# A graph layer's two projections regrouped: neighbour half alone first, self half beside each tile's aggregation

## The reference

```python
Wi, Wj = (W[:, :Din], W[:, Din:])
mi = jnp.einsum('bkd,od->bko', x, Wi)
mj = jnp.einsum('bkd,od->bko', x, Wj)
a = adj.astype(x.dtype)
deg = a.sum(axis=1)
out = deg[None, :, None] * (mi + b) + jnp.einsum('ij,bjo->bio', a, mj)
...
x = _layernorm(x + _L0_gnn_ref(x, adj, L0_gnn_W, L0_gnn_b), axis=-1)
```

## Time and profile before

| | |
|---|---|
| median of 3 runs | 1643.62 us (1643.59 to 1643.74) |
| the profiled execution, own time | 1643.72 us |
| its span in the profile | 1641.9 us |
| TensorE busy | 1634.2 us |
| VectorE, ScalarE, GpSimd busy | 844.8, 661.7, 498.4 us |
| moved by DMA | 187.27 MB |

### The profile page before, as it was taken

The page is one execution under the profiler, slowest core; times in us unless marked ns, Lnnn a source line. Parts: engine busy times, 40 slices in busy tenths (PEclk is TensorE's granted clock), DMA queues, the critical chain, the costliest instruction groups (busy, mean ns, idle before and its releaser), DMA issues.

```text
span 1641.9 us, 24654 instructions
## 1 busy us (share of the span) xinstructions
PE 1634.2 (100%) x7196; PEld 1346.8 (82%) x7196; DVE 844.8 (51%) x1879; ACT 661.7 (40%) x964; POOL 498.4 (30%) x386
## 2 busy tenths in 40 slices
PE   9999999999999999999999999999999999999998
PEld 6888888888888888888888888888888888888886
DVE  8787644554444544444544544444544454544544
ACT  5765445332453324532245332452325522255221
POOL 3532134311343114431144211442114421144210
PEclk9999999999999999999999999999999999999999
DMA  6676422332234323243223332233323333233332
GB/s 205 193 226 223 141 84 94 131 108 96 83 102 133 100 93 96 89 134 109 84 95 101 123 115 83 95 114 117 102 83 102 124 106 106 74 101 115 96 115 70
DMA packets 102843, 187.27 MB, mean 114 GB/s; under 512 B 11424, under 2 KB 11680, under 8 KB 102816
## 3 DMA queue, kind: packets, MB, share of 16 engines
q1 hardware_dynamic: 84672, 154.05, 29.1%
q10 hardware_dynamic: 18144, 32.91, 6.3%
HBM read 119.80 MB, written 67.11 MB: 114 GB/s over the span
## 4 chain that ended last, share of the span: by engine, by line
PE 98%; DVE 1%; DMA 0%; issue 0%; POOL 0%; ACT 0%; DVEq 0%
PE agg_ps L375 57%; PE cross_ps L343 14%; PE main_ps L351 14%; PE main_ps L353 14%; DVE W_lo L558 0%; DVE W_df L561 0%; DMA mi_in<-in_wt 0%; DVE adjT L555 0%; DVE x_raw L579 0%; DVE mj_lo L568 0%; PE deg_ps L360 0%; POOL x_df L281 0%; DVE x_top L576 0%; DVE stats L630 0%; DVE r L628 0%
## 5 line engine op out<-in xcount | busy, mean ns | idle before, releaser
L375 PE MATMUL agg_ps<-mj_hi,adjT 128*128 128x512 f32 x2048 | 797.0, 389 | 0.0
L375 PE MATMUL agg_ps<-mj_lo,adjT 128*128 128x512 f32 x2048 | 796.7, 389 | 0.0
L470 ACT ACTIVATE adjT<-adjT 128x2048 fp32r (+1 forms) x128 | 245.4, 1917 | 562.8 <-PE agg_ps L375 562.8
L375 PEld LDWEIGHTS agg_ps<-mj_hi,adjT 128*128 128x128 f32 x2048 | 384.5, 188 | 79.9
L375 PEld LDWEIGHTS agg_ps<-mj_lo,adjT 128*128 128x128 f32 x2048 | 384.3, 188 | 79.7
L351 PE MATMUL main_ps<-W_hi,x_hi 128*128 128x512 f32 x1008 | 392.3, 389 | 0.0
L353 PE MATMUL main_ps<-W_lo,x_lo 128*128 128x512 f32 x1008 | 392.1, 389 | 0.0
L292 POOL TENSOR_TENSOR mi_in<-mi_in,bias 128x512 f32<-128x512 f32 x128 | 166.9, 1307 | 649.9 <-DMA mi_in<-mi_dram 649.9
L628 DVE TENSOR_TENSOR r<-agg_ps,r 128x512 f32<-128x512 f32 x128 | 88.6, 692 | 355.0 <-PE agg_ps L375 354.9
L343 PE MATMUL cross_ps<-W_df,x_df 128*128 128x512 f32 x1008 | 270.2, 390 | 0.6 <-DVE W_df L561 0.5
L286 POOL TENSOR_TENSOR mj_lo<-mj,mj_hi 128x512 f32 (+1 forms) x126 | 166.7, 1323 | 323.4 <-ACT mj_hi L458 323.4
(11 more groups left out here) (59 smaller groups left out, 592.1 us busy)
## 6 DMA issues: line engine op xcount, KB each, us to landing
mi_dram<-mi SPq DMA_DIRECT2D x128, 256.0 KB, 2.1
mi_in<-mi_dram SPq DMA_DIRECT2D x128, 256.0 KB, 2.7
r<-in_x SPq DMA_DIRECT2D x128, 256.0 KB, 2.6
out<-r SPq DMA_DIRECT2D x127, 256.0 KB, 2.1
x_raw<-in_xt ACTq DMA_DIRECT2D x124, 256.0 KB, 2.7
adj_in<-in_adjt SPq DMA_DIRECT2D x64, 256.0 KB, 3.9
r<-in_wt SPq DMA_DIRECT2D x4, 256.0 KB, 5.2
adj_in<-in_xt SPq DMA_DIRECT2D x2, 256.0 KB, 4.0
```

The source lines that it names most:

```text
L375: last = nc.tensor.matmul(agg_ps[s][:, :], adjT[s][:, j, :], part[:, j, :], start=(j == 0 and part is mj_hi), stop=(j == NT - 1 and part i ...
L470: nc.scalar.activation(adjT[s][:, :, :], adjT8[:, :, bass.ds(i * P, P)], ACT.Copy).then_inc(adjT_ready, 1)
```

## The change

A batch becomes 32 steps (STEPS). Steps 0 to 15 project the neighbour half of tiles 0 to 15. Step 16 + i projects the self half of tile i, and the aggregation of tile i follows on TensorE at once. mi stays in SBUF, in two buffers; x is loaded and split once for each step, so twice a tile. x_hi is now ScalarE's rounding of x itself; VectorE makes the rest and x_df (two instructions with two SBUF operands), ScalarE x_lo; GpSimd keeps mj_lo and the bias. x_raw has four buffers, mj and cross two. Only the neighbour halves of tiles 0 and 1 are projected in plain fp32. W is rounded by ScalarE first; VectorE splits the self half of W at tiles 3, 5, 7 and 9 of batch 0. The adjacency comes by row tile, four chunks a tile, widened straight into adjT and kept as int8 afterwards (`keep`); one reduce and one fp32 matmul a tile give deg. The body of a batch, looped over batches 1 to 6, is written out without inner loops.

```diff
-            def store_mi(n):
-                sp.wait_ge(mi_ready, n + 1)
...
+                    sp.wait_ge(x_lo_ready, q)
+                    sp.wait_ge(x_df_ready, q)
+                    sp.dma_start(x_raw[(t + 5) % 4][:, :], xt[base + (t + 5) % NT]).then_inc(x_loaded[(t + 5) % 4], 16)
...
-            def difference(n, s):
-                pool.wait_ge(x_parts_ready, 2 * (n - NATIVE) + 2)
-                pool.tensor_tensor(x_df[s][:, :], x_top[:, :], x_lo[s][:, :].bitcast(fp32),
-                                   ALU.subtract).then_inc(x_df_ready, 1)
...
+            def add_bias(q, i):
+                pool.wait_ge(comb_ready, q + 1)
+                pool.tensor_tensor(mi[i % 2][:, :], mi[i % 2][:, :], bias[:, :], ALU.add).then_inc(mib_ready, 1)
...
+            def project(q, st, zero):
+                s = st % 2
+                half = 1 if st < NT else 0
...
+                pe.wait_ge(x_df_ready, q - NATIVE + 1)
+                if not (zero and st < 2 * NATIVE):
+                    pe.wait_ge(cross_ready, q - 2 * NATIVE + 1)
...
+            def degree(i):
+                pe.wait_ge(deg_part_ready, i + 1)
+                if i:
+                    pe.wait_ge(deg_ready, i)
+                nc.tensor.matmul(deg_ps[:, 0:2], deg_part[i % 2][:, :], ones[:, :],
+                                 start=True, stop=True).then_inc(deg_in_psum, 1)
...
+                        project(STEPS * bt + t, t, zero)
+                for i in range(NT):
+                    if zero:
+                        degree(i)
+                    project(STEPS * bt + NT + i, NT + i, zero)
+                    aggregate(bt, i, zero)
...
-            for h in range(2):
-                for n in range(NATIVE):
-                    project_native(n, h)
+            for n in range(NATIVE):
+                project_native(n)
...
+            def round_x(q, st, turn):
+                act.wait_ge(x_loaded[st % 4], turn)
+                act.wait_ge(main_done, q - 1)
+                nc.scalar.activation(x_hi[st % 2][:, :], x_raw[st % 4][:, :], ACT.Copy).then_inc(x_hi_ready, 1)
...
+            def scale_x(q, st):
+                act.wait_ge(x_rest_ready, q - NATIVE + 1)
+                nc.scalar.activation(x_lo[st % 2][:, :], x_raw[st % 4][:, :], ACT.Copy, scale=S).then_inc(x_lo_ready, 1)
...
+            def widen_chunk(c):
+                i, k = c // 4, c % 4
+                act.wait_ge(adj_loaded[c % AB], 16 * (c // AB + 1))
...
+                nc.scalar.activation(adjT[i % 2][:, 4 * k:4 * k + 4, :],
+                                            adj_in[c % AB][:, :].rearrange("p (a d) -> p a d", a=4),
+                                     ACT.Copy).then_inc(adj_wide, 1)
+
+            def keep(i):
+                act.wait_ge(adj_wide, 4 * i + 4)
+                nc.scalar.activation(adjT8[:, :, i * P:(i + 1) * P], adjT[i % 2][:, :, :].bitcast(fp32),
+                                     ACT.Copy).then_inc(adj_kept, 1)
...
-            copy_w_hi(0, DK)
+            round_x(2, 2, 16)
+            round_w(0)
+            scale_x(2, 2)
             native_mj_hi(1)
...
+            round_x(3, 3, 16)
+            for c in range(1, DK):
+                round_w(c)
+            act.wait_ge(w_ready, DK)
+            load_x(4, 4)
+            load_x(5, 5)
+            scale_x(3, 3)
...
+                def step(st, middle):
+                    q = first_step + st
+                    take_cross(q, st)
...
+                        round_x(q + 2, st + 2, x_turn(bt, st + 2))
+                    if middle:
+                        top_of_mj(q, st)
+                    if ahead:
+                        scale_x(q + 2, st + 2)
+                    if not middle and not (final and st + 5 >= STEPS):
+                        act.wait_ge(x_df_ready, q)
+                        load_x(base + (st + 5) % STEPS % NT + (NT if st + 5 >= STEPS else 0), st + 5)
...
+                    if zero:
+                        keep(i)
+                    if not (final and i >= NT - 2):
+                        act.wait_ge(agg_done, m + 1)
+                        if zero and i + 2 < NT:
+                            for k in range(3):
+                                widen_chunk(4 * (i + 2) + k)
                             root(m)
...
+                            widen_chunk(4 * (i + 2) + 3)
...
+            def split_x(q, st):
+                dve.wait_ge(x_hi_ready, q - NATIVE + 1)
+                nc.vector.tensor_tensor(x_raw[st % 4][:, :], x_raw[st % 4][:, :], x_hi[st % 2][:, :].bitcast(fp32),
                                         ALU.subtract).then_inc(x_rest_ready, 1)
...
+                dve.wait_ge(x_rest_ready, q - NATIVE + 1)
+                nc.vector.scalar_tensor_tensor(x_df[st % 2][:, :], x_raw[st % 4][:, :], -S,
+                                               x_hi[st % 2][:, :].bitcast(fp32),
+                                               ALU.mult, ALU.add).then_inc(x_df_ready, 1)
...
+            def combine(q, st, into):
+                dve.wait_ge(main_done, q + 1)
+                dve.wait_ge(cross_ready, q - NATIVE + 1)
...
+            def count(i):
+                dve.wait_ge(adj_wide, 4 * i + 4)
...
+                nc.vector.tensor_reduce(deg_part[i % 2][:, :],
+                                        adjT[i % 2][:, :, :].rearrange("p j i -> p i j").bitcast(fp32),
+                                        AX.X, ALU.add).then_inc(deg_part_ready, 1)
...
-                split_w(DK + order, order)
+                split_w(W_ORDER[order], order)
+            split_x(2, 2)
...
-            split_x(NATIVE, 0, 16)
-            for order in range(1, DK):
-                split_w(order, DK + order)
...
+                    combine(q, t, mj[t % 2])
+                    split_x(q + 2, t + 2)
+                    if zero and t in (3, 5, 7, 9):
+                        order = DK + (t - 3) // 2
+                        split_w(W_ORDER[order], order)
                 if zero:
+                    count(0)
+                for i in range(NT):
+                    m, q = base + i, first_step + NT + i
+                    combine(q, NT + i, mi[i % 2])
+                    if not (final and i >= NT - 2):
+                        split_x(q + 2, i + 2)
+                    if zero:
+                        if i + 1 < NT:
+                            count(i + 1)
+                        take_degree(i)
+                    residual(m, i, bt, zero)
+                    normalise(m, i % GT, i % 2, final and i == NT - 1)
```

More of the change, by code:

```diff
@@ L48, in sem @@
             return ctx.enter_context(nc.semaphore(name))
-        mi_dram = nc.dram_tensor("mi_dram", [TILES, P, DO], fp32, kind="Internal").ap()
         adjT8 = sb("adjT8", [P, NT, N], i8)
@@ L58, in bass_adj_resnorm @@
         W_df = sb("W_df", [P, 2 * DK, DO], fp32r)
-        x_raw = [sb(f"x_raw{s}", [P, D], fp32) for s in range(2)]
-        x_top = sb("x_top", [P, D], fp32)
+        x_raw = [sb(f"x_raw{s}", [P, D], fp32) for s in range(4)]
         x_hi = [sb(f"x_hi{s}", [P, D], fp32r) for s in range(2)]
@@ L354, in project @@
                                             W_lo[:, half * DK + k, :], start=False, stop=(k == DK - 1))
                 last.then_inc(main_done, 1)
-            def degrees(q):
-                pe.wait_ge(deg_part_ready, NT * (q + 1))
-                for t in range(TPB):
-                    last = nc.tensor.matmul(deg_ps[:, 2 * t:2 * t + 2], deg_part[q % 2][:, t * P:(t + 1) * P], ones[:, :],
-                                            start=True, stop=True)
-                last.then_inc(deg_in_psum, 1)
```

586 lines of the change are left out of this document (174 added, 412 removed).

## The result

The changed kernel takes 1700.52 us in the median (1699.82 to 1702.03), the kernel before 1643.61 (1643.48 to 1643.74) beside it: ratio 1.0347, with a 95% interval of 1.0335 to 1.0359. It is 57 us slower; forecast were 1661 us and at most 1697.

The account below looks back on a forecast made before the run. TensorE was taken as the bound, busy 1634.2 of 1641.9 us. A span of 1639.7 us without waits plus 19.6 us of waits gave 1659.3, with 1.8 us around it 1661; range 1649 to 1697.

Parts of the forecast that it names:

- start of the first batch: First batch's start: TensorE waits 0.5 us after the native fp32 projections, then 2.9 us for x_df behind tile 4's late fetch.
- W's self half, four tiles: Batch 0, tiles 3, 5, 7, 9: VectorE gets 1.33 us more where 0.5 to 0.7 is free; 5.1 us of waits.
- eight adjacency chunks: Tiles 8 to 15, ScalarE: each chunk adds 0.53 us, its loop closes in 3.0 instead of 2.72; 1.8 us of waits.
- TensorE's own work: Whole kernel: fewer native fp32 passes, 7144 split matmuls, degree matmuls 0.2 us each; span without any wait 1639.7 us.
- Tile 4's late fetch: First batch: fetch queued on ScalarE behind W rounding lands at 16.75; x_df at 19.9, wanted at 17.0, 2.9 us late.
- GpSimd in that beat: First stage: VectorE's x_df and GpSimd's mj_lo start within 0.03 us and exclude each other; VectorE was taken first.
- The rival of 1693: Looped batches: GpSimd first, TensorE waits 0.65 us every second tile, 32 us in seven batches; 1693 us, chance 0.27.
- The first degree matmul: Ahead of first self projection: VectorE's reduce begins at 2.1, takes 2.3 us; TensorE waits until 4.4 us (ends 3.3, 5.7).
- Later tiles have 9.97 us for about 8 of VectorE: First batch's later row tiles: VectorE needs about 8 us, ScalarE 6.5, of 9.97 us; they wait for nothing.
- From batch to batch: Turns: first combine queues behind last normalisation, x_df(2) ready at 6.12, wanted at 5.44; 0.7 us seven times, 4.9 us.
- a rival, of 2 us at six turns: Batch loop's jump: code is refetched, some 2 us at each of six turns, 12 us; 1673 us, chance 0.2.
- its own sign: Wrong in the main if a looped batch's first stage exceeds 44.3 us, or the first batch loses under 8 us.

## Why the prediction failed, step by step

Waits in us, worked out from the starts of the projections in the changed kernel's trace (the execution of 1702.03 us) against 2.72 a projection and 9.97 a row tile:

| term | predicted | measured |
|---|---|---|
| start of the first batch | 0.5 + 2.9 | 2.1 |
| W's self half, four tiles | 5.1 | 5.3 |
| eight adjacency chunks | 1.8 | 1.9 |
| wait ahead of the first degree matmul | 4.4 | 7.1 |
| 14 later row tiles of the first batch (11.26 each against 9.97 + 0.2) | 0 | 15.3 |
| seven turns | 4.9 | 15.8 |
| half clock, behind the first degree and four turns | 0 | 2.6 + 6.9 |
| small slips, of some 0.14 us a restart, and one of 0.94 | 0 | 3.5 |
| in all | 19.6 | 60.5 |

- *TensorE's own work* was right: with the span of 1700.2 and 60.5 us of waits it is again 1639.7. Only the degree matmul costs 0.25 and not 0.2.
- *Start, W's self half, adjacency chunks* were right in sum (9.3 against 10.3), read from rows alone. Tile 4's late fetch was over-rated: all of the start cost 2.1 us, and issuing it earlier gave 0.2 us in one kernel and nothing in the other. That is within the start's own variation: tile 4's delay is 0.4 us in this trace, but 1.6 and 2.0 in two kernels whose start is unchanged (those with the count in the order of memory and with short loops). So the near agreement of this sum is partly luck.
- *GpSimd in that beat*: VectorE is first, as taken, in every looped batch, and x_df stays at 0.69 us there. It was about as close as the forecast's 0.03 us said: x_df starts 0.04 to 0.12 us ahead of GpSimd's mj_lo, so that the choice was right is in part luck. The rival of 1693 didn't come; its time lies near the result by accident. Once, in the last batch, GpSimd does come first (1529.60, x_df 1529.77): x_df takes 1.68 us there and TensorE waits 0.8, near the 0.65 that the rival set for such a tile.
- *The first degree matmul* failed by size, in two parts. I took 2.3 us for the reduce and it is 3.60 here, because of the stride. And I let it begin 2.1 us after the last projection where it began 3.2 us after, since the combine three instructions ahead of it waited 1.07 us for ScalarE's cross, which stands behind the widening of an adjacency chunk (58.92 to 59.53). The bounds from the rows of before, 1.2 to 2.3, didn't hold it: none of those rows has a stride, and I had not looked at the access pattern.
- *"Later tiles have 9.97 us for about 8 of VectorE"* is the step that failed most. Row by row VectorE has 11.2: 1.5 more for the reduce, 1.0 because x_df meets GpSimd's bias, and some 0.7 in a sum that I had rounded down instead of adding up. The margin that I saw was not there, and 15.3 us hang on it.
- *From batch to batch*: the 0.7 us a turn was the right mechanism (0.4 measured where the turn is reached in line). Added to it is the fetch, 2.6 us at five of the seven. I had it as a rival, of 2 us at six turns, and gave it 0.2. It showed at the third projection, through VectorE's x_df, and not at a batch's first matmul, where I had looked for it: TensorE's own back jump, over 896 rows, leaves no gap there. By its own sign the prediction is wrong in the main: the first stage of the looped batches that a back jump leads into lasts 46.7 to 48.7 us, over the 44.3 that it set.
- *What no part had*: TensorE's clock. A gap was priced at its own length, but behind five gaps of 2.63 to 6.68 us a stretch of 1.2 GHz follows, 1.7 to 2.6 us more each, 9.5 in all.

What stays open: why the clock fell behind four of the five back jumps and not behind the first; why VectorE goes on 1.6 us after the first instruction packet has landed and not at once; and what makes the 0.6 us at the turn of the short loops, of which a short jump elsewhere costs only 0.2.

## What to carry to other kernels

When work moves from a stage with two projections a tile to one with a single, add up the receiving engine's rows one by one, its collisions with GpSimd too; a margin of a rounded 2 us was in truth 1.2 us short, in tile after tile. A reduce along a stride is priced apart from a contiguous one, and its one operand makes it the instruction to lay beside GpSimd's. A loop body made long by unrolling is paid at its back jump, so put that jump where the engine waits anyhow, and keep TensorE's gaps short, since the clock may add 1.7 us or more to one of 2.5.

## What was not expected of the hardware

- A reduce of 128x2048 fp32 takes 3.79 us with 512-byte steps and 2.27 us contiguous; of 512 elements with the same step 1.07 us.
- VectorE's jump back over a batch's code costs 2.6 us, with an instruction packet of 8 KB in the pause; a jump over four tiles costs 0.2 us and fetches nothing.
- Behind idle stretches of 2.63 to 6.68 us TensorE's matmuls came 0.43 us apart, at a granted clock of 0.50; behind others of 2.63, 2.74 and, in another kernel, 3.09 us they came at 0.2267. The length of the gap alone doesn't decide it.
- Instructions of VectorE with two SBUF operands, started behind a GpSimd instruction, took 1.79 us in place of 0.69 in ten tiles running.
